# Two hybrid attention layers on one core: where the keys' and values' lengths, the output parts and the last chunks stand in a kernel's slot table

## The reference

```
x = x + attention_a(layernorm(x))     # plain causal softmax attention, q, k, v, o projections
x = x + ffn(layernorm(x))             # r = sigmoid(W_r xr), k = relu(W_k xk)^2, out = r * (W_v k)
x = x + attention_b(layernorm(x))
x = x + ffn(layernorm(x))

# attention_b, per head, on 16 channels
k = decayed running sum of (x @ W_k.T) along the tokens
k = k / (norm(k) + 1e-10) * key scale
v = (1 - v_coef) * shift(x @ W_v.T) + v_coef * (x @ W_v.T)     # the mixing
v = v / (norm(v) + 1e-10) * value scale
y = softmax(causal(q . k)) @ v, with q = k one token later; y @ W_c.T
```

## Time and profile before

| | |
|---|---|
| median of three executions | 3010.07 us (3009.12 to 3013.25) |
| the profiled execution | 3010.78 us, span 3009.1 us |
| PE busy | 2862.4 us, 95% of the span |
| ACT busy | 2232.7 us, 74% |
| DVE busy | 1472.8 us, 49% |
| POOL busy | 817.1 us, 27% |
| granted PE clock, mean | 0.976 |

### The profile page before, as it was taken

The page is one execution under the profiler, slowest core; times in us unless marked ns, Lnnn a source line. Parts: engine busy times, 40 slices in busy tenths (PEclk is TensorE's granted clock), DMA queues, the critical chain, the costliest instruction groups (busy, mean ns, idle before and its releaser), DMA issues.

```text
span 3009.1 us, 99722 instructions
## 1 busy us (share of the span) xinstructions
PE 2862.4 (95%) x42984; PEld 1302.0 (43%) x42984; DVE 1472.8 (49%) x3579; ACT 2232.7 (74%) x2487; POOL 817.1 (27%) x1246
## 2 busy tenths in 40 slices
PE   6999999999999899998999999999999989999897
PEld 3444444444444344444444444444444434444343
DVE  5322346565556654445344434555665656523544
ACT  2799978787787478784788878778787856788472
POOL 4222223332323222221222222232333322322111
PEclk9999999999999899998999999999999999999898
DMA  5322312222222123222322223222222221222111
GB/s 136 106 83 81 95 53 78 70 73 67 81 71 60 52 67 103 81 76 67 95 81 74 82 89 94 64 78 68 63 75 71 73 66 52 72 72 85 41 62 41
DMA packets 229828, 225.34 MB, mean 75 GB/s; under 512 B 33221, under 2 KB 212933, under 8 KB 229320
## 3 DMA queue, kind: packets, MB, share of 16 engines
q1 hardware_dynamic: 228504, 217.47, 25.3%
q10 hardware_dynamic: 816, 0.79, 0.1%
HBM read 146.80 MB, written 71.32 MB: 72 GB/s over the span
## 4 chain that ended last, share of the span: by engine, by line
PE 72%; DVE 16%; issue 6%; ACT 4%; POOL 1%; SPq 0%; DVEq 0%; DMA 0%; ACTq 0%
PE ps L872 46%; PE ps L1103 23%; ACT probs L828 4%; DVE pmax L1434 3%; PE ps L884 3%; DVE xn L1198 2%; DVE nw_y L1180 1%; DVE nw_u L1178 1%; DVE ln_st L1186 1%; DVE nw_u L1176 1%; DVE x_buf L1315 1%; DVE o_blk L1493 1%; DVE k_blk L1413 1%; DVE nw_v L1389 1%; POOL buf_k L703 0%
## 5 line engine op out<-in xcount | busy, mean ns | idle before, releaser
L828 ACT ACTIVATE probs<-ps 128x1024 f32<-128x1024 f32 x2176 | 2083.1, 1059 | 477.7 <-PE ps L872 474.5
L872 PE MATMUL ps<-q_st,k_st 99*32 99x512 bf16 (+3 forms) x20480 | 1237.4, 349 | 5.0 <-issue 2.4
L1103 PE MATMUL ps<-probs,v_st 128*17 128x512 f32 (+3 forms) x10240 | 1160.7, 532 | 22.4 <-POOL probs L731 13.1
L872 PEld LDWEIGHTS ps<-q_st,k_st 99*32 99x32 bf16 x20480 | 567.0, 96 | 775.7 <-issue 449.6
L731 POOL TENSOR_SCALAR_AFFINE_SELECT probs<-probs 128x256 f32<-128x256 f32 (+1 forms) x896 | 433.4, 501 | 1138.7 <-ACT probs L828 1120.1
L1103 PEld LDWEIGHTS ps<-probs,v_st 128*17 128x17 f32 x10240 | 291.9, 98 | 272.2 <-issue 59.1
L872 PE MATMUL ps<-xT,wT 128*32 128x512 f32 x2048 | 242.6, 594 | 0.0
L1493 DVE STREAM_TRANSPOSE o_blk<-ps 128x512 f32<-128x512 f32 x128 | 91.0, 711 | 269.2 <-PE ps L1103 268.9
L657 POOL TENSOR_TENSOR parts<-rest,parts 128x512 bf16<-128x512 f32 x96 | 120.9, 1260 | 316.7 <-DVE parts L1221 316.7
L1348 DVE SCALAR_TENSOR_TENSOR buf_v<-buf_v,ps 128x512 f32<-128x512 f32 x64 | 44.0, 687 | 272.9 <-PE ps L872 272.9
L1315 DVE TENSOR_TENSOR x_buf<-x_buf,ps 128x512 f32<-128x512 f32 x64 | 43.8, 684 | 217.6 <-PE ps L872 207.2
(11 more groups left out here) (140 smaller groups left out, 2148.9 us busy)
## 6 DMA issues: line engine op xcount, KB each, us to landing
part_a<-parts SPq DMA_DIRECT2D x192, 128.0 KB
x_buf<-in_L_attn_a_X SPq DMA_DIRECT2D x32, 512.0 KB, 4.6
q_st<-part_a SPq DMA_DIRECT2D x128, 128.0 KB
o_chan<-o_out SPq DMA_DIRECT2D x64, 256.0 KB, 2.4
o_in<-o_chan SPq DMA_DIRECT2D x64, 256.0 KB, 4.6
q_st<-part_b SPq DMA_DIRECT2D x128, 128.0 KB
k_st<-part_a SPq DMA_DIRECT2D x64, 192.0 KB, 2.9
part_b<-parts SPq DMA_DIRECT2D x96, 128.0 KB
```

What stands on the lines that cost most here:

```text
L828: nc.scalar.activation(probs[:, g % NP_BUF, :], ps[:, bk:bk + 2, :].rearrange("p a n -> p (a n)"), ACT.Exp, scale=SCALE[ATT[g // (NHG * NG ...
L872: last = pe.matmul(o[c:c + 32], kt[:, c:c + 32], q, **how)
L1103: last = pe.matmul(ps[32 * j:32 * j + VW, bank, q0:q0 + w], v_st[:, k % 2, kb, hg * HG + j, :], p, start=(kb == 0), stop=(kb >= TB * qc), ...
```

## The change

Five things are changed.

1. In T_M the output parts `o0`, `o1` stand two slots sooner (S - 6 and S - 4), and their loads too.
2. The lengths block is cut in two. The keys' half, 64 wide, with the scaling of the keys behind it, stands at offset 58, behind the mixing. The values' half, 64 wide, stands at offset 73, which is slot S + 1 of the next head group, and POOL's scaling of the values at offset 82. POOL's difference in the next job now waits for the keys' sum alone.
3. In the first P jobs the norm stands 5 slots sooner and the loads 6; the first x chunk is loaded alone: SP waits for it before it issues the second chunk and the weights.
4. The last four jobs start at slots 10, 24, 45 and 69 of the last head group, in place of 16, 37, 58 and 82. Their output chunks are loaded 4 slots ahead of the start, not 10.
5. The last output transposition writes into `o_in` directly, so its store and its load go.

```diff
-T_P0 = {"load": -10, "ln": 0, "t0": 6, "t1": 8, ...
+T_P0 = {"load": -16, "ln": -5, "t0": 6, "t1": 8, ...
-T_M = {"load": -10, "o0": 0, "o1": 2, "ln": 3, "t0": 12, "t1": 14, ...
+T_M = {"load": -12, "o0": -2, "o1": 0, "ln": 3, "t0": 12, "t1": 14, ...
-       "len": 63, "keys": 69, "split": 91, "vb": 70, "low": 94, "store": 98}
+       "klen": 58, "vlen": 73, "split": 91, "vb": 82, "low": 94, "store": 98}
+T_LAST = {**T_END, "o_load": -4}
-    jobs += [Job("MB", 3, c, 7, start(7, 3) + (16, 37, 58, 82)[c], T_END) for c in range(NCH)]
+    jobs += [Job("MB", 3, c, 7, start(7, 3) + (10, 24, 45, 69)[c], {**T_LAST, "load": -4} if c == 2 else T_LAST) for c in range(NCH)]
...
+                    if j is LAST_JOB and m == KT - 1:
+                        continue
...
-            for c in range(2):
-                load_x(JOB["P", 0, c])
+            load_x(JOB["P", 0, 0])
+            sp.wait_ge(s_x[0], 16)
+            load_x(JOB["P", 0, 1])
...
-                    pool.wait_ge(s_vfac, [i for i in earlier if i.kind == "MA"][-1].at["ma"] + 1)
+                    pool.wait_ge(s_ksum, [i for i in earlier if i.kind == "MA"][-1].at["ma"] + 1)
...
+                        if j is LAST_JOB:
+                            pe.wait_ge(s_o_in, 32 * f + 16)
+                            pe.wait_ge(s_ot, len(ATT) * KT * NCH)
...
-                yield j.t0 + j.off["len"]
+                yield j.t0 + j.off["klen"]
...
+                sums(buf_a, of_keys).then_inc(s_ksum, 1)
+                dve.wait_ge(s_ksum, j.at["ma"] + 1)
+                inverse_lengths(of_keys)
...
+                yield j.t0 + j.off["vlen"]
                 dve.wait_ge(s_vsq, 2 * (j.at["ma"] + 1))
+                step(sums(buf_k, of_values))
+                settle()
+                inverse_lengths(of_values)
...
+                    if sg == NI * NCH - 1:
+                        dve.wait_ge(s_part, JOBS[-2].at["o1"].n + 1)
+                        dst = o_in[:, KT - 1, :]
```

More of the change, by code:

```diff
@@ L119 @@
        "flag": 31, "store": 4}
-T_P0 = {"load": -10, "ln": 0, "t0": 6, "t1": 8, "u0": 14, "u1": 16, "u2": 18, "u3": 20, "v0": 22, "v1": 24, "n": 28,
+T_P0 = {"load": -16, "ln": -5, "t0": 6, "t1": 8, "u0": 14, "u1": 16, "u2": 18, "u3": 20, "v0": 22, "v1": 24, "n": 28,
         "flag": 31, "store": 4}
@@ L237 @@
 JOB = {(j.kind, j.b, j.c): j for j in JOBS}
+LAST_JOB = JOB["MB", B - 1, NCH - 1]
+assert LAST_JOB is JOBS[-1]
 def stored(u):
@@ L370, in hybrid_kernel @@
         s_ksq = sem("key_squares")
+        s_ksum = sem("key_squares_summed")
         s_w1 = sem("value_weighted")
@@ L455, in m_job @@
                 load_x(j)
+                if "o_load" in j.off:
+                    yield j.t0 + j.off["o_load"]
                 load_o(j)
@@ L574, in main @@
                 n, i = divmod(slot - 2, NG)
-                if 0 <= n < NI and i in LAST_OF and n % 2:
+                if 0 <= n < NI and i in LAST_OF and n % 2 and (n, i) != (NI - 1, NG - 1):
                     store_o(n * NCH + LAST_OF.index(i))
-            for c in range(2):
-                load_x(JOB["P", 0, c])
+            load_x(JOB["P", 0, 0])
+            sp.wait_ge(s_x[0], 16)
+            load_x(JOB["P", 0, 1])
             for i in (FR, FK, FV, BK, BV):
@@ L1167, in settle, with rsqrt @@
                 dve.wait_ge(s_dve, steps[0])
-            def rsqrt(n):
-                v, y, w = nw_v[:, 0:n], nw_y[:, 0:n], nw_u[:, 0:n]
+            def rsqrt(at):
+                v, y, w = nw_v[:, at], nw_y[:, at], nw_u[:, at]
                 step(nc.vector.tensor_scalar(y.bitcast(I32), v.bitcast(I32), 1, None, ALU.arith_shift_right))
@@ L1181, in rsqrt, with sums @@
                     settle()
+            def sums(sq, at):
+                return nc.vector.tensor_reduce(nw_v[:, at], sq[:, :, :].rearrange("p k (g e) -> p (k g) e", e=DK), AX_X, ALU.add)
+            def inverse_lengths(at):
[3 more added lines that the diff above has]
+                step(nc.vector.tensor_tensor(nw_u[:, at], nw_v[:, at], nw_y[:, at], ALU.mult))
+                settle()
+                step(nc.vector.tensor_scalar(nw_u[:, at], nw_u[:, at], NORM_EPS, None, ALU.add))
+                settle()
+                step(nc.vector.reciprocal(nw_y[:, at], nw_u[:, at]))
+                settle()
             def statistics(j, first, end):
@@ L1195, in normalize @@
                 settle()
-                rsqrt(TB)
+                rsqrt(slice(0, TB))
                 for tb in range(TB):
@@ L1251, in p_job @@
             def p_job(j):
-                yield j.t0
+                yield j.t0 + j.off["ln"]
+                if j.b == 0 and j.c:
+                    dve.wait_ge(s_part, JOB["P", 0, j.c - 1].at["t1"].n + 1)
                 x_there(j)
@@ L1391, in m_job @@
[L1391 to L1400, removed]
@@ L1401, in m_job @@
-                nc.vector.tensor_tensor(v_fac[:, :].rearrange("p (t h) -> p t h", t=TB),
-                                        nw_y[:, nh:2 * nh].rearrange("p (t h) -> p t h", t=TB),
-                                        v_scale[:, :].unsqueeze(1).to_broadcast([P, TB, H]),
-                                        ALU.mult).then_inc(s_vfac, 1)
-                fac = nw_v[:, 0:nh]
+                of_keys, of_values = slice(0, nh), slice(nh, 2 * nh)
+                sums(buf_a, of_keys).then_inc(s_ksum, 1)
@@ L1409, in m_job @@
                                              .to_broadcast([P, KT, BL, 2]), ALU.mult))
-                yield j.t0 + j.off["keys"]
                 settle()
@@ L1414, in m_job @@
                 settle()
+                yield j.t0 + j.off["vlen"]
+                dve.wait_ge(s_vsq, 2 * (j.at["ma"] + 1))
+                step(sums(buf_k, of_values))
+                settle()
+                inverse_lengths(of_values)
+                nc.vector.tensor_tensor(v_fac[:, :].rearrange("p (t h) -> p t h", t=TB),
+                                        nw_y[:, of_values].rearrange("p (t h) -> p t h", t=TB),
+                                        v_scale[:, :].unsqueeze(1).to_broadcast([P, TB, H]),
+                                        ALU.mult).then_inc(s_vfac, 1)
                 yield j.t0 + j.off["split"]
```

18 lines of the change are left out of this document (8 added, 10 removed).

## The result

The changed kernel takes 3091.11 us (median of 4; before 3009.82, median of 4): ratio 1.0266, 95% interval 1.0246 to 1.0286. One of the four executions fell in a slow state (3160.61 us at a mean granted clock of 0.917) and is left out of the ratio; the other three have a median of 3089.87. It is slower, as forecast, but by 80 us and not by 44: the time lies 7 to 8 us above the range that I gave, whose upper end was 3083.

The account below looks back on a forecast made before the run. PE's single queue, 95% busy, was taken as the bound. Terms +72 - 43.3 + 16.5 + 7 - 5 - 3 gave +44.2 us, so 3054 us against the median, range 3006 to 3083.

Parts of the forecast that it names:

- V: DVE time of the values' half (17 instructions) between the norm and the take that `t0` needs: 5.5 us, from 4.3 to 8.0.
- the sum: All terms added over the whole kernel: +44.2 us, giving 3054 us against the median.
- `t0`'s wait, +72: PE at `t0` waits for DVE's delayed take of the last chunk: 4.5 us on average at sixteen boundaries, +72 us.
- +7 for the pause: DVE's 3.28 us instruction-fetch pause behind the flag's branch delays the take: 2.0 us at 7 boundaries, halved to +7 us.
- The clock, +16.5: PE works slower at 1.2 GHz after new boundary stalls: 1.5 us at each of eleven, +16.5 us (0 to 24).
- The removed waits, -43.3: PE's boundary waits for `o1`, the next product and `t0` all vanish: 45.7 us less 2.4 in the tail.
- the paragraph on the rivals: Supported the slower forecast (chance 0.75): `t0` already waits for this take at 14 of 16 boundaries, leaving no slack.
- The head, -5: At the start, earlier norms recover waits for `xn` though parameters come 1.7 us later: -5 us (-8 to 0).
- The tail, -3: At the end, less work after the last product, but more ahead of it and `o0` waits: -3 us (-13 to +6).
- its dear end: Upper end for the whole kernel, with V at 8.0 us and full clock and pause costs: 3109 us.
- The rival that the block is covered: At `t0`, 3.5 of the values' half's 5.5 us are hidden, leaving 1.0 us waits: 2975 us; chance 0.17.

Follow-up runs that it names:

- run 12: The changed kernel with 100 one-column memsets ahead of everything on DVE, so that its later code stands 100 places further: 3100.91 us (one execution).
- run 6: The changed kernel with only the values' sum at offset 63, its chain at 86, POOL's scaling at 90, output parts and loads at old slots: 2968.57 us, ratio 0.9857.
- run 4: The kernel before with only the changed head and tail, lengths block and output parts as before: 3007.85 us, ratio 0.9990.
- run 8: The changed kernel with fourteen pieces of the values' half done twice, some 4.2 us more DVE work: 3161.27 us (one execution).
- run 1: The changed kernel with the values' half at offset 63 in place of 73, ahead of the output parts' additions: 3058.78 us, ratio 1.0161.
- run 2: The changed kernel with the values' half at offset 63 and the output parts and loads at their old slots: 3015.81 us, ratio 1.0016.
- run 3: The changed kernel with only the output parts and loads back at their old slots, values' half still at 73: 3099.16 us, ratio 1.0291.
- run 5: The changed kernel with the values' half at offset 81, behind the take and first copy, and POOL's scaling at 86: 3091.29 us (one execution).

## Why the prediction was wrong

The mechanism was right: the values' half stood on the one chain that `t0` waits for, with nothing that covers it. The direction, the place and V (5.5 forecast, 5.49 measured) held; in V two small errors cancel (the fourteen pieces took 3.51 and not 3.64, and the last instruction, which the sum leaves out, added 0.14). The failed step is the sum; its largest mis-sized terms are `t0`'s wait and the clock, 12 and 11 us too small.

- **`t0`'s wait, +72 and +7 for the pause.** Measured 91.3 us over sixteen boundaries. Some 8 of the 12 us come from the distance from take to `t0`. I had it from two boundaries, 6.80 and 7.24; over all sixteen it is 6.66 to 7.79 without V, 7.35 in the mean, and PE was there 0.09 sooner at the first boundary. So the ten boundaries without a long pause wait 4.6 to 5.1 and not 4.2 to 4.8. The other six wait 6.6 to 7.6. I had bounded the pause at 2 us in seven boundaries and then halved it; it came out at 41.7 less six times 5.1, 11 us, nearly whole. Halving a known pause because its places might change was unfounded: run 12 shows that it moves and does not go.
- **The clock, +16.5.** Measured 27.4 us of longer work in the two stretches. I took 1.5 us for each of eleven new stalls. The three old ones were right, but the clock fell at all sixteen boundaries and not at fourteen, so thirteen were new, 2.1 us each. Run 6, with no such stall, is busy 34 us less than the changed kernel, 2.2 for each of the sixteen. Both lie within the 1.7 to 2.6 of the earlier trace rows. My own rows had the price, and I went below it.
- **The removed waits, -43.3.** At the sixteen boundaries they were 36.1 in the trace before. I had let all waits of the earlier trace rows but 2.4 us go, also those that stand elsewhere in the run. Nor does `t0` wait at 14 of the 16 boundaries, as the paragraph on the rivals has it: the fourteen waits are those of the whole run, and ten stand at these boundaries.
- **The head, -5.** -5.2 up to head group 2, -4.3 from head group 3; the first instruction that needs the parameters starts at 15.66 against 14.19, 1.5 later (1.7 forecast). That it came so close is in part luck, since it varies as run 4 says.
- **The tail, -3.** +2.9. Behind the last take it is 11.8 us shorter (13.5 forecast), but the head group ahead of it 14.8 longer (10.7 forecast), with waits of 12.3 us in place of 6.0: `o0` behind its DMA 3.4 and 2.0, `k0` behind DVE 2.5.

The differences of these terms, 12.3, 10.9, 7.2, 0.7 and 5.9, make up the 37 between 44 and the 81.5 of the two traces. All erred on the same side, which my range had not allowed for: its dear end, worked out as 3109, I had cut to 3083.

The rival that the block is covered falls with the sixteen waits and with run 8. What I had not asked is whether the block could stand anywhere: kept whole, the kernel is 5 to 89 us slower than before at each place that was tried (runs 1, 2, 3, 5); with the half cut where the data binds it is 42 us faster (run 6).

## What to carry to other kernels

Before moving a block on a secondary engine, list that engine's idle stretches over one whole period and the latest point that each of the block's inputs allows; then cut it where the data binds (here the sum), not where its outputs part. An idle stretch read right behind a stall is partly that stall's echo and can't be spent. Cutting a chain of narrow instructions in two by width does not halve its parts: a piece of 64 columns took 0.23 us where one of 128 took 0.29.

## What the runs showed of the hardware

- A stall of PE of 4.9 us was followed by about 6 us at a granted clock of 0.50, and such a stall cost some 2 us of longer work; one of 8.8 us (run 8) cost hardly more on top. Before the change, waits of 2.1 to 2.6 us were followed by 3.4 us at 0.50 at three boundaries and by none at three others.
- DVE's `TENSOR_TENSOR` on 64 columns takes 0.23 us against 0.29 on 128 and 0.16 on 4, its reciprocal 0.55 against 0.95 on 128: only the reciprocal goes nearly by width.
- A 0.23 us DVE piece with two inputs in SBUF took 1.00 when it met a 1.04 us POOL instruction, and one of 0.69 took 1.82 when it met one of 1.93.
- The pause of 3 to 4 us behind a branch stood at the same repeats in four traces of the same DVE code, on two chips, and moved to other repeats when the program was shifted by 100 instructions.
